# Loading X in four transfers of four tiles, with the first statistics taken quarter by quarter, in a four-layer graph attention kernel

## What is computed

```python
def reference(x, adj, ...):
    h = relu(layernorm(x));  x = x + multi_head_gat(h, adj, W_heads, a1, a2) @ W_out + b_out   # 8 heads, elu
    h = relu(layernorm(x));  x = x + gelu(gat(h, adj, W, r))
    h = relu(layernorm(x));  x = x + elu(gat(h, adj, W, a))
    h = relu(layernorm(x));  x = x + elu(gat(h, adj, W, a))
    return x

def gat(h, adj, W, a):            # all in float32
    Wh = h @ W
    e = leaky_relu((Wh @ a1)[:, None] + (Wh @ a2)[None, :], 0.2)
    att = softmax(where(adj > 0, e, -big), axis=1)
    return att @ Wh
```

## Time and profile before

| | us |
|---|---|
| median of three runs | 768.17 |
| profiled execution, own time | 767.65 |
| its span | 766.0 |
| outside the span | 1.65 |
| TensorE busy | 745.2 (97%) |
| VectorE busy | 628.0 (82%) |
| ScalarE busy | 327.6 (43%) |

### The profile page before, as it was taken

The page is one execution under the profiler, slowest core; times in us unless marked ns, Lnnn a source line. Parts: engine busy times, 40 slices in busy tenths (PEclk is TensorE's granted clock), DMA queues, the critical chain, the costliest instruction groups (busy, mean ns, idle before and its releaser), DMA issues.

```text
span 766.0 us, 15942 instructions
## 1 busy us (share of the span) xinstructions
PE 745.2 (97%) x6443; PEld 727.3 (95%) x6443; DVE 628.0 (82%) x1050; ACT 327.6 (43%) x886; POOL 16.1 (2%) x36
## 2 busy tenths in 40 slices
PE   8899999999999999999999999999889989998997
PEld 8789999999999999999999999999779979996997
DVE  4997879797787968879787797878688959997986
ACT  5876551452543336134354324633440254435420
POOL 3000000000000000000000000000000000000000
PEclk9999999999999999999999999999999999999999
DMA  9794000000000000000000000000000000000001
GB/s 298 263 357 186 29 28 2 27 0 27 27 1 27 0 27 3 24 27 0 27 12 15 27 0 27 0 0 1 2 1 2 1 1 1 2 1 1 1 22 36
DMA packets 13874, 29.39 MB, mean 38 GB/s; under 512 B 1296, under 2 KB 7568, under 8 KB 13840
## 3 DMA queue, kind: packets, MB, share of 16 engines
q1 hardware_dynamic: 11152, 20.00, 7.6%
q0 software_dynamic: 2688, 8.92, 3.3%
HBM read 27.80 MB, written 1.11 MB: 38 GB/s over the span
## 4 chain that ended last, share of the span: by engine, by line
PE 85%; ACT 5%; DVE 5%; DMA 3%; issue 1%; POOL 0%; DVEq 0%; ACTq 0%; POOLq 0%
PE acc L408 49%; PE acc L431 25%; PE side L508 3%; PE side L364 3%; DMA stage<-in_adj_t_dram 3%; ACT adjT L623 2%; PE acc L378 1%; PE acc L482 1%; DVE probs L1082 1%; ACT hpT L716 1%; PE side L470 1%; DVE stats L1284 0%; PE side L456 0%; DVE xn L1328 0%; ACT fill L701 0%
## 5 line engine op out<-in xcount | busy, mean ns | idle before, releaser
L408 PE MATMUL acc<-V,probs 128*128 128x129 f32 x3840 | 438.3, 276 | 1.9 <-DVE probs L1076 1.9
L408 PEld LDWEIGHTS acc<-V,probs 128*128 128x128 f32 x3840 | 434.2, 192 | 4.9 <-ACT V L657 2.7
L1082 DVE SCALAR_TENSOR_TENSOR probs<-rho,t_now,adjT 128x1024 f32<-128x1024 f32 x224 | 272.9, 1277 | 11.3 <-PE acc L408 9.1
L1178 DVE SCALAR_TENSOR_TENSOR probs<-rho,t_now,adjT 128x768 f32<-128x768 f32 (+3 forms) x179 | 146.7, 879 | 9.6 <-PE acc L431 6.6
L716 ACT ACTIVATE hpT<-rows 32x256 f32<-32x256 f32 x224 | 92.8, 414 | 69.5 <-DVE rows L1119 67.0
L431 PEld LDWEIGHTS acc<-stage,probs 128*128 128x128 f32 x1024 | 115.0, 192 | 4.0 <-ACT stage L874 3.7
L431 PE MATMUL acc<-stage,probs 128*128 128x129 f32 x1024 | 116.1, 275 | 2.1 <-DVE probs L1178 2.1
L431 PE MATMUL acc<-V,probs 128*128 128x129 f32 x768 | 89.4, 275 | 1.0 <-DVE probs L1178 1.0
L431 PEld LDWEIGHTS acc<-V,probs 128*128 128x128 f32 x768 | 87.4, 192 | 2.0 <-ACT V L874 1.8
L701 ACT ACTIVATE fill<-mean_now,empty 128x128 f32<-128x128 f32 x120 | 36.7, 394 | 87.9 <-DVE den L1095 87.8
L1127 DVE TENSOR_TENSOR X<-X,side 128x512 f32<-128x512 f32 x28 | 19.3, 688 | 63.5 <-PE side L508 63.5
(11 more groups left out here) (190 smaller groups left out, 409.4 us busy)
## 6 DMA issues: line engine op xcount, KB each, us to landing
stage<-in_adj_t_dram SPq DMA_DIRECT2D x32, 512.0 KB, 6.7
rho<-rho_dram POOLq DMA_DIRECT2D x15, 512.0 KB, 3.7
X<-in_x_dram SPq DMA_DIRECT2D x2, 512.0 KB, 4.5
W0t<-in_W_t_dram SPq DMA_DIRECT2D x1, 512.0 KB, 5.2
W<-in_L_gnn_W_heads_dram SPq DMA_DIRECT2D x1, 512.0 KB, 6.4
Wout<-in_L_gnn_W_out_dram POOLq DMA_DIRECT2D x1, 512.0 KB, 9.3
out_dram<-X SPq DMA_DIRECT2D x1, 512.0 KB, 4.5
out_dram<-X SPq DMA_DIRECT2D x1, 384.0 KB, 3.9
```

Source lines behind the costliest of these rows:

```text
L408: last = nc.tensor.matmul(group(c, k), probs[:, j % RING, k * P:(k + 1) * P], V[:, j, :], start=(j == 0 and k % PER_BANK == 0), stop=(j == ...
L1082: nc.vector.scalar_tensor_tensor(probs[:, j % RING, :], rho[:, c * CH:(c + 1) * CH], t_now[:, j:j + 1], adjT[:, j, c * CH:(c + 1) * CH], A ...
L1178: return nc.vector.scalar_tensor_tensor(slot_of(n, p, j)[:, first:end], rho[:, at + first:at + end], t_now[:, j:j + 1], adjT[:, j, at + fi ...
```

## The change

X is loaded by four transfers of four tiles (256 KB each) in place of two of eight (512 KB each), each with a semaphore of its own. VectorE waits for each quarter just before its first tile, in place of waiting for each half. The aggregation of the statistics stays by halves. GpSimd waits for the last quarter where it waited for the second half.

```diff
-        x_in = [sem(f"x_in{c}") for c in range(2)]
+        x_in = [sem(f"x_in{q}") for q in range(4)]
...
         @block.sync
         def _(sp):
-            for c in range(2):
-                sp.dma_start(X[:, c * NK:(c + 1) * NK, :], x_v[:, c * NK:(c + 1) * NK, :]).then_inc(x_in[c], 16)
+            for q in range(4):
+                sp.dma_start(X[:, 4 * q:4 * q + 4, :], x_v[:, 4 * q:4 * q + 4, :]).then_inc(x_in[q], 16)
             sp.dma_start(a0_sb[:, :, :], a0).then_inc(w0t_in, 16)
...
-            pool.wait_ge(x_in[1], 16)
+            pool.wait_ge(x_in[3], 16)
...
                 for c in range(2):
-                    dve.wait_ge(x_in[c], 16)
                     for k in range(c * NK, (c + 1) * NK):
+                        if k % 4 == 0:
+                            dve.wait_ge(x_in[k // 4], 16)
                         last = nc.vector.bn_stats(stats[:, k, :], X[:, k, :])
```

## The result

The changed kernel is slower by a little. Twenty runs of each gave a median of 768.81 us against 767.63, a ratio of 1.0014 with a 95% interval of 1.0007 to 1.0020. The medians are 1.2 us apart, and the interval is 0.5 to 1.5 us. (Of the runs of before that are used further down, one at 1288.78 us is left out everywhere.) The profiled execution took 769.23 us with a span of 767.5, 1.5 us above that of before.

What follows compares the result with a forecast made beforehand. TensorE was taken to bound the kernel (745.2 of 766.0 us), the opening by the weights' branch. Gain 0 and loss 0 left 767.65 us profiled, plus 0.52 to the median: 768.2 us, range 767.0 to 769.5.

Steps and rivals of the forecast that it cites:

- What bounds the opening: Before ScalarE's norming: X's branch ends at 10.74 us, the weights' branch at 10.78, so the weights' branch sets the start.
- What the change removes: Opening, VectorE: quarters land near 3.8, 4.7, 5.6 and 6.5 us, so the inverse root ends 0.78 us earlier.
- What of it reaches the end: At ScalarE's norming, still waiting for line 523: a gain between 0 and 0.04 us, taken as 0.
- A shift of the opening is carried one to one: From ScalarE's norming on, through the first two units to the third's projection at 81.88 us: any opening shift persists whole.
- What it adds: On SyncE, two more issues ahead of other loads, moving W0t's issue from 3.45 to 4.41-4.69 us; loss taken as 0.
- the term of W0t: Opening, line 523: loss from W0t landing later, taken as 0 because queued bytes hide its later issue.
- My upper bound: Most that W0t's later landing could cost at line 523: the whole issue delay, 0.96 to 1.24 us.
- The adjacency stream: Loads for ScalarE's casts: issued up to 1.24 us later but covered, the first waiting cast being at 39.56 us.
- The sum: Whole kernel: gain 0 and loss 0 on 767.65 us profiled, plus 0.52 to the median, giving 768.2 us.
- The second rival: Line 523: W0t lands late, costing one to one up to 1.24 us; 768.2 to 769.4 us, chance 0.17.
- The third rival: TensorE idles 1.24 us at 8.7 us, then a low clock costs 1.87; 3.1 us in all, 771.3 us, chance 0.03.
- my fourth rival: Loads of X: the transfers' fixed part does not overlap, so W0t lands 4.0 us later; 772.2 us, chance 0.01.

Runs made afterwards that it cites:

- e5: Changed kernel with ScalarE norming before copying line 523's products, line 523 moved between the transpositions, 30 identity matmuls ahead; ratio 1.0006 to the kernel before.
- e6: Kernel before, X in two transfers, with norming ahead of the copies, and line 523 moved between the transpositions; ratio 1.0006 to the kernel before.
- e9: Changed kernel with norming before the copies, line 523 still ahead of the transpositions, 27 identity matmuls ahead and none behind; ratio 1.0001 to the kernel before.
- e10: Kernel before, X in two transfers, with norming before the copies, 27 identity matmuls, line 523 ahead of the transpositions; ratio 0.9996 to the kernel before.
- e4: The changed kernel run again unaltered, for a second trace; ratio 1.0013 to the kernel before.
- e1: Changed kernel, but VectorE waits for both quarters of a half before its statistics; 768.89 us against 768.73 for the changed kernel, ratio 1.0021 to the kernel before.
- e2: Kernel before with two added 8 KB loads of a0 on SyncE behind X's two transfers, ahead of W0t; ratio 1.0004 to the kernel before.
- e3: Changed kernel with W0t issued right behind the four quarters, W0s behind it, a0 through GpSimd's queue; ratio 1.0015 to the kernel before.
- e11: Changed kernel with X in three transfers, of four, four and eight tiles; ratio 1.0010 to the kernel before.
- e12: Changed kernel with the second and fourth quarters issued by ScalarE, the first and third by SyncE; ratio 1.0007 to the kernel before.
- e7: The kernel before run again unaltered, for a second trace; no ratio given, W0t landed at 8.70 us and line 523 started at 8.78.
- e8: Changed kernel with 27 identity matmuls in place of 20 ahead of line 523; ratio 1.0008 to the kernel before.

## Why the prediction was off by what it was

- **What bounds the opening: right.** Two branches meet on ScalarE, and the weights' branch is the later. ScalarE's idle time ahead of the copy grew as said. e5 and e6 show the other half: with W0t away, the norming follows the inverse root.
- **What the change removes: right in kind, wrong in size.** The first two quarters landed at 3.87 and 4.66 us as worked out (3.8, 4.7). The last two landed at 6.30 and 7.54, where I had 5.6 and 6.5. I had spaced four landings by the distance of two, and the trace of before has no third large transfer on the queue from which that could have been read. So the inverse root came 0.12 us earlier in place of 0.78 in the first trace. The size varies: in the pairs e5 and e6, e9 and e10 it is 0.6, and in e4 ScalarE's first estimate of the inverse root starts at 8.52 us, 0.84 earlier than before.
- **What of it reaches the end: right, nothing.** e1, without the quarters' waits, has the time of the changed kernel.
- **A shift of the opening is carried one to one: not borne out.** I held that ScalarE's chain, which sets the third unit, moves with the opening. In e6 and e10 the opening is 0.9 and 1.2 us later than in before and the third unit 1.2 earlier. The chain runs through the adjacency stream, which I had left out of it.
- **What it adds: wrong, and this is the step that failed.** I took the term of W0t at 0, since the queue of bytes ahead would hide the later issue. That mechanism holds (e2: 1.08 us of delay cost 0.18). But it assumed that the DMA engines go on at 279 to 296 GB/s. With the third and fourth quarters they fell to 207 and then to about 173 GB/s, and W0t landed 1.39 us later in the profiled execution and 0.5 to 1.4 in the eight traces. The bytes alone do not make up the 1.39: from 2 to 8 us the engines moved 258 GB/s on the mean against 287 before, 0.17 MB less, which by an estimate from these rates is 0.6 us. And in e3 they moved 283, with W0t 0.54 us late. What else holds W0t up is open. My upper bound, 1.24, was worked out from the issue alone and is just too low, though W0t's issue moved by only 0.60 us (3.45 to 4.05).
- **The adjacency stream: wrong.** I called it covered, by where before first waits (39.56 us). In four of eight traces a cast waited 0.5 to 2.8 us for it before 30 us, and in e1 and e11, which waited 2.79 and 2.00, the third unit starts latest (84.72 and 84.02). How much of the 1.2 us is W0t's landing and how much is these pieces, no run separates.
- **The sum.** 768.2 was forecast and 768.81 measured, inside the range of 767.0 to 769.5, though a term was wrong. That is in part luck: the median of the three runs I started from, 768.17, lay 0.54 above that of twenty, which hid nearly half of the 1.2 us. The second rival, W0t late and one to one, is the nearest to what happened: it said 768.2 to 769.4, and had a chance of 0.17. One to one is not shown. Its condition (the first byte ready later than 5.9 us) came true by another way than its own, the slow transfers. The third rival's dearer end happened in part: the clock fell behind the wait. It was priced at 1.87 us a stretch, by 0.112 us a record, and costs 1.43, since the 32 records without it take 4.02 us and not 3.58. In the first trace that stretch was then missing over the first unit, in e4 it was not.
- **The fixed cost of a transfer.** The rule of the Trainium skill (DMA: Bandwidth & Descriptors, Anatomy of one DMA) that each transfer carries a fixed cost of about 2.0 us was weighed and set aside. It has the direction right, where my term was 0, but not the size: by my fourth rival W0t would land 4.0 us later, and it landed 1.39 later. It misses for each transfer too: two small transfers more cost 0.18 us (e2), and two large ones on another queue cost nothing in W0t's landing (e12).

## What to carry to other kernels

Before a load at the head of a queue is split, look at what stands behind it in the same queue, and at how many large transfers are already in flight there. Here two of X were free and a third was not, though whether their number or the bytes ahead decide is open. The one that paid was the load in front of which TensorE had no work left. A gain on one of two branches that meet within 0.04 us is worth nothing until the other branch is shortened too, and it took a second trace of the same kernel (e7) to see that the tie was one execution's. And a shift at the head of a kernel is to be followed to the point where the next engine joins: here ScalarE's chain through the adjacency stream, and not TensorE's own start, sets the third unit in before and after.

## What the runs showed of the hardware

- A third large transfer on SyncE's queue moved its bytes late. In e11 the engines fell to 98 GB/s at 4.0 to 4.5 us, once the first two (256 KB each) were through, though the third had been issued at 1.90 us. In the seven traces with four quarters on one queue they fell to 206 to 267 GB/s there, and in the one trace with two queues they stayed at 318. The Trainium skill (DMA: Bandwidth & Descriptors, Issuing engines are not separate DMA queues) says that starting transfers from several engines at once only saves the time it takes to initiate them. e12 differs: against the changed kernel it moved W0t's landing from 9.16-10.04 to 8.62, and e2 shows that the issue time is worth 0.18 us of that. The measurement decides. What in the queue holds the third back (a limit on what is in flight, or the making of descriptors) stays open, and so does why W0t trails by 2.8 us behind W0s in e8, where X itself had landed by 6.54.
- TensorE's slow start (a record of an identity matmul every 0.21 us, then every 0.11) ended between about 4.6 (e2) and 7.8 us (e1) from execution to execution, with a granted clock of 1.00 in the rows throughout. So the end of 20 identity matmuls lies anywhere in a stretch of 1.5 us.
- A stretch of low clock, 0.50 (the 1.2 GHz level) for 3.4 us, costs 1.43 us over the first unit (5.45 against 4.02 for 32 records). It falls at other places from run to run, and with the mean clock in the fit the spread of a single run falls from 0.9 to 0.6 us.
